# Attention pass of a graph kernel: turned one-hots compared from broadcast offset rows, exponentials also in PSUM, next scores placed earlier on TensorE

## Chip, cores and metric
One core of one Trainium2 chip runs the whole program. The metric is the device time of one execution in microseconds (us). Five engines work side by side: TensorE (PE, its weight loads PEld), VectorE (DVE), ScalarE (ACT), GpSimd (POOL) and SyncE (SP), which issues DMAs.

## What is computed
Four graph layers run on 6250 nodes of 128 features and 200,000 edges sorted by target. Only the third, an attention layer with 4 heads, is changed:

```python
h_src, h_tgt = h[src], h[tgt]
att = jnp.sum(jnp.concatenate([h_src, h_tgt, e], axis=-1) * a, axis=-1)
att = jnp.where(att > 0, att, 0.2 * att)
m = jnp.maximum(segment_max(att, tgt), 0.0)
ex = jnp.exp(att - m[tgt])
denom = segment_sum(ex, tgt) + (num_edges - deg)[:, None] * jnp.exp(-m)
out = segment_sum((ex / denom[tgt])[:, :, None] * h_src, tgt)
```

## The kernel before
`attention_pass` takes the edges in 196 groups of 1024 (128 partitions times J = 8 slots), written out four at a time (U = 4 buffers, so 49 rounds). Targets are sorted, so the targets of a group lie in a window of 128 nodes. Each engine has its own program, and a `step` function says in which order it takes the parts of neighbouring groups. Semaphores tie the engines together. Within step g:

- **POOL** gathers the 1024 source rows of a group by 8 indirect DMAs (L2885). It may refill a buffer when `weigh` has used it (`weighed`), so it gathers group g+3 once group g-1 is weighed, and the group's indices must have been loaded.
- **SP** issues, group by group, the loads of the edge features `e64`, of the window's table `ht` and of the gates `gate` (L2864, L2867, L2869), each waiting until the same buffer's last user four groups earlier is done, and after each round the four index loads (L1195).
- **ACT** makes the one-hots "edge i has target w" in `make_hots` fashion three groups ahead: 8 instructions of distances, one Relu to bf16 (`hots`, L3247), a widening to f32 (`widen_hots`, L3256). It copies the turned one-hots out of PSUM (`take_hots`, L3265) and the turned edge features (`take_edges`, L3273), takes the sums (`take_sums`, L3300), and makes the exponentials (`weights`, L3292).
- **PE** turns the one-hots (`turn_hots`, L3106), multiplies turned edges and one-hots into scores (`score_edges`, L3131 and L3133), turns the run ends and the carries (`turn_ends`, `turn_carries`), and sums the weighted rows of the last group in two halves (`sum_rows`, L3171).
- **DVE** adds the parts of a score, runs the segmented maxima, carries them over partitions, subtracts, and in `weigh` (L3065) multiplies the gathered rows by the exponentials.

PE's order in a step is: first half of the last group's sums, run ends, second half of those sums, carries, scores of the next group, turned edges and one-hots of the group after, scale, sums turned. DVE's order ends with differences, `close_tops`, `sum_scores(nxt)` (L2922, waits for the next group's scores) and `weigh(g)`. ACT's order is: edges and one-hots of the next group, half of the distances, `take_sums(last)`, `weights(g)`, then the rest.

`weights_stage` prepares weights early in the program, long before. `Passes` keeps a window's offsets.

## Time and profile before

| | us |
|---|---|
| median of 3 runs | 7490.35 (7471.94 to 7496.29) |
| the profiled execution's own time | 7530.3 |
| its span | 7528.5 |
| the attention pass in it, from its first sums to its last (L3171) | 3863.4 to 6571.4 |

In the rows, a time at the start of a line of the timeline is us from the span's start, the second number is the busy time of that row, and square brackets hold the idle time of the engine just before it with what ended it. "remote" stands where the event that ended a wait could not be put down to an instruction's end. "issue" means that nothing the profile shows was waited for. PE records carry the modelled end of the arithmetic, not the moment when the semaphore was seen by others.

### The profile page before, as it was taken

How to read it: one execution, taken by the hardware profiler on the slowest of the kernel's cores; microseconds unless marked ns; L12 is line 12 of the kernel's file. 1: busy time of each engine (PE TensorE's matmuls, PEld its weight loads, DVE VectorE, ACT ScalarE, POOL GpSimd, SP SyncE). 2: the span in 40 equal slices, each digit the busy share in tenths (PEclk: the TensorE clock that was granted, in tenths of full speed). 3: DMA queues.
4: the chain of work that ended last, by engine and by line, in shares of the span. 5: the costliest groups of instructions: out<-in, count | busy, mean ns of one | idle time of the engine just before them, and what ended most of it. 6: DMA issues, size and time to landing. Idle time of an engine off the chain costs nothing. (4 is left out here: it accounts for less than half of the span.)

```text
span 7528.5 us, 95690 instructions
## 1 busy us (share of the span) xinstructions
PE 4397.0 (58%) x27040; PEld 3669.2 (49%) x27040; DVE 2592.7 (34%) x8505; ACT 2302.1 (31%) x5410; POOL 4035.3 (54%) x4085
## 2 busy tenths in 40 slices
PE   3288883445544555544445655565655655548887
PEld 2155552445544545544434544555554554435555
DVE  5876553111111111111244333333333433441214
ACT  0233443111111111111144544444444444420002
POOL 0266653566666666666345555555555555446660
PEclk6599995777777777777756566656656556669896
DMA  3133332111111111111122222222222222144441
GB/s 54 38 117 128 137 127 72 42 46 48 45 44 44 48 46 47 46 43 45 29 58 58 57 63 56 62 58 57 63 56 62 58 57 61 44 131 138 143 144 38
DMA packets 363838, 510.15 MB, mean 68 GB/s; under 512 B 200192, under 2 KB 258774, under 8 KB 352657
## 3 DMA queue, kind: packets, MB, share of 16 engines
q0 software_dynamic: 129536, 268.78, 14.3%
q1 hardware_dynamic: 234137, 239.31, 10.4%
q8 instruction: 87, 1.43, 0.1%
q14 instruction: 78, 0.64, 0.0%
HBM read 416.50 MB, written 91.05 MB: 67 GB/s over the span
## 5 line engine op out<-in xcount | busy, mean ns | idle before, releaser
L2885 POOL DMA_INDIRECT rows_l<-table,idx_l x1568 | 1496.8, 955 | 1255.1 <-issue 1028.2
L2527 POOL DMA_INDIRECT rows_l<-table,idx_l x1568 | 1565.2, 998 | 918.1 <-issue 761.9
L3171 PE MATMUL p_sum_l<-wrow_l,hot_l 128*128 128x136 f32 x3136 | 789.5, 430 | 1092.0 <-DVE wrow_l L3065 1092.0
L2663 PE MATMUL ps_l<-hoty_l,rows_l 128*128 128x144 f32 x3136 | 688.3, 399 | 1147.2 <-DVE hoty_l L2595 863.5
L3171 PEld LDWEIGHTS p_sum_l<-wrow_l,hot_l 128*128 128x128 f32 x3136 | 717.4, 325 | 1186.8 <-issue 871.3
L1475 POOL DMA_INDIRECT rows_l<-table,row_idx x896 | 934.1, 1043 | 543.4 <-issue 250.9
L2663 PEld LDWEIGHTS ps_l<-hoty_l,rows_l 128*128 128x128 f32 x3136 | 631.2, 284 | 1190.1 <-DVE hoty_l L2595 653.0
L2611 DVE TENSOR_TENSOR acc<-acc,pw_l 128x128 f32 x196 | 56.6, 289 | 2048.4 <-DMA counts_table<-h_nodes 1157.6
L2549 ACT COPY agg_l<-ps_l 128x432 f32<-128x432 f32 (+1 forms) x588 | 276.0, 479 | 1436.3 <-PE ps_l L2663 849.7
L2676 PE MATMUL pm_l<-w_mix,agg_l 128*128 128x128 f32 x3528 | 517.1, 307 | 43.2 <-issue 42.9
L2676 PEld LDWEIGHTS pm_l<-w_mix,agg_l 128*128 128x128 f32 x3528 | 501.9, 225 | 48.9 <-issue 46.6
L3236 ACT ACTIVATE apart_l<-iota,rel_s_l 128x128 bf16<-128x128 f32 x1568 | 497.2, 387 | 10.1
L1730 PE MATMUL pa_l<-pieces_l,x_nodes 128*128 128x384 bf16 x2254 | 453.6, 338 | 26.2 <-issue 23.9
L1730 PE MATMUL pa_l<-pieces_l,h_nodes 128*128 128x384 bf16 x2156 | 432.6, 339 | 28.6 <-issue 23.0
L2922 DVE TENSOR_REDUCE score_l<-bank_s_l 128x32 f32<-128x128 f32 x196 | 57.4, 293 | 1112.0 <-remote 1102.8
L1716 PE MATMUL pc_l<-hot_key_l,hot_lo_l 128*128 128x392 bf16 (+1 forms) x1152 | 288.2, 313 | 195.4 <-issue 81.3
L1730 PEld LDWEIGHTS pa_l<-pieces_l,x_nodes 128*128 128x128 bf16 x2254 | 223.7, 101 | 177.5 <-issue 54.3
L1591 DVE TENSOR_TENSOR hot_lo_l<-lo_iota_l,tile_lo 128x512 bf16<-128x512 bf16 x288 | 198.6, 690 | 323.8 <-PE pc_l L1716 246.1
L1730 PEld LDWEIGHTS pa_l<-pieces_l,h_nodes 128*128 128x128 bf16 x2156 | 214.5, 101 | 180.5 <-issue 56.4
L1593 DVE TENSOR_SCALAR hot_key_l<-key_iota_l,key_l 128x392 bf16<-128x392 f16 (+1 forms) x1152 | 291.7, 307 | 0.0
L2595 DVE TENSOR_TENSOR hoty_l<-hot_l,y_l 128x1152 f32<-128x1152 f32 x196 | 266.5, 1360 | 13.2 <-PE ps_l L2663 6.5
L2560 ACT COPY msg_l<-pm_l 128x128 f32<-128x128 f32 x196 | 52.6, 268 | 711.5 <-DMA x_nodes<-in_x 394.1
(552 smaller groups left out, 7041.3 us busy)
## 6 DMA issues: line engine op xcount, KB each, us to landing
rows_l<-table,idx_l POOLq DMA_INDIRECT x3136
e_l<-in_edge_attr SPq DMA_DIRECT2D x196, 256.0 KB
counts_table<-x_nodes SPq DMA_DIRECT2D x22, 1568.0 KB
x_nodes<-counts_table SPq DMA_DIRECT2D x22, 1568.0 KB
counts_table<-h_nodes SPq DMA_DIRECT2D x21, 1568.0 KB
h_nodes<-counts_table SPq DMA_DIRECT2D x21, 1568.0 KB
rows_l<-table,row_idx POOLq DMA_INDIRECT x896
raw_l<-in_edge_attr SPq DMA_DIRECT2D x49, 144.0 KB
```

What stands on the lines that cost most here:

```text
L1475: pool.indirect_dma_start(out=rows[:, slot, j, :], out_offset=None, in_=table, in_offset=bass.IndirectOffsetOnAxis(ap=what[:, j:j + 1], ax ...
L1593: nc.vector.tensor_scalar(hot_key[:, f % RING, 0:near_keys], key_iota[:, 0:near_keys], key[:, t:t + 1], None, ALU.is_equal).then_inc(tile_ ...
L1716: nc.tensor.matmul(pc[m % BANKS][:, at:at + near_keys], hot_lo[:, f % RING, :], hot_key[:, f % RING, 0:near_keys], start=(k % per == 0), s ...
L1730: last = nc.tensor.matmul(pa[n % 2][:, 0:PIECES * D], counts[n % BUFFERS][:, a, :], pieces[:, a, :, :].rearrange("p k d -> p (k d)"), star ...
L2527: pool.indirect_dma_start(out=rows[:, u, j, :], out_offset=None, in_=table, in_offset=bass.IndirectOffsetOnAxis(ap=idx[:, u, j:j + 1], axi ...
L2549: nc.scalar.copy(agg[:, s, :, a:b, :], ps[n][:, 0:(b - a) * Y * RANGE].rearrange("p (t c d) -> p c t d", c=Y, d=RANGE)).then_inc(part_take ...
L2595: nc.vector.tensor_tensor(hoty[:, s, :, :, :], hot[:, s, :, :].unsqueeze(2).broadcast_to([P, J, Y, RANGE]), y[:, :, u * J:(u + 1) * J].rea ...
L2663: last = nc.tensor.matmul(ps[n][:, at:at + Y * RANGE], rows[:, u, t, :], hoty[:, s, t, :, :].rearrange("p c d -> p (c d)"), start=True, st ...
L2676: last = nc.tensor.matmul(pm[s][:, 0:D], agg[:, s, c, :, :].rearrange("p t d -> p (t d)"), w_mix[:, c, :], start=(c == 0), stop=(c == Y - 1))
L2885: pool.indirect_dma_start(out=rows[:, u, j, :], out_offset=None, in_=table, in_offset=bass.IndirectOffsetOnAxis(ap=idx[:, u, j:j + 1], axi ...
L3171: last = nc.tensor.matmul(p_sum[:, 0:WROW], hot[:, s, j, :], wrow[:, s, j, :], start=(j == 0), stop=(j == J - 1))
L3236: last = nc.scalar.activation(apart[:, j, :], core.iota[:, :], ACT.Abs, scale=-1.0, bias=rel_s[:, g.s, j:j + 1])
```

## The change
The turned one-hots no longer come from PE. `weights_stage` once turns the targets' offsets (13 PE transposes into PSUM, ACT copies to 16-bit integers, two DMAs) into a table `rel_rows` in DRAM, one row of 1024 numbers per group. SP loads a group's row into all 128 partitions, and DVE compares it with each partition's own line number, which gives the turned one-hots at once. ACT's bf16 one-hots, the widening copy and the copy of turned ones go, and the one-hots are written once in f32, one group ahead. The exponentials are written twice, first into PSUM for `weigh`, then into the rows for the sums. PE makes the scores of the next group and the carries before the second half of the last group's sums.

```diff
# weights_stage
+        rel = sb("rel_kept", [P, T])
+        rel_row = sb("rel_row", [P, len(chunks), P], I16)
+        pr = ctx.enter_context(nc.psum_tensor("pr", [P, 4, 512], F32))
...
+            sp.wait_ge(rel_taken, START + 1)
+            rows = core.rel_rows.rearrange("g (j p) -> (g j) p", p=P)
+            sp.dma_start(rows[0:full * P, :].rearrange("(c k) p -> k c p", k=P), rel_row[:, 0:full, :]).then_inc(rel_stored, DMA)
+            sp.dma_start(rows[full * P:T, :], rel_row[0:T - full * P, full, :]).then_inc(rel_stored, DMA)
             sp.wait_ge(loaded, START + n * DMA)
+            sp.wait_ge(rel_stored, START + 2 * DMA)
...
+            nc.vector.tensor_scalar(rel[:, :], core.rel0[:, :, :].rearrange("p g j -> p (g j)"), -1.0, None, ALU.max).then_inc(rel_kept, 1)
...
+            for c, (at, k) in enumerate(chunks):
+                turned = nc.tensor.transpose(pr[0:k, c // 4, c % 4 * P:c % 4 * P + P], rel[:, at:at + k], core.ident[:, :])
# Passes
+        link(nc.vector.tensor_tensor(self.mine[:, :], self.line_far[:, :], self.off[:, :], ALU.add))
...
+        nc.vector.tensor_tensor(self.line_far[:, :], core.line[:, :], core.order[:, 1:2], ALU.subtract)
# attention_pass
-        hot_b = sb("hot_b", [P, U, J, WIN], BF16)
+        rel_row = sb("rel_row", [P, J * P], I16)
-        p_hotT = ctx.enter_context(nc.psum_tensor("p_hotT_l2", [P, J, P], BF16))
+        p_ex = psum("p_ex", 512)
+        ex = p_ex[:, 0:2 * Q].rearrange("p (s j h) -> p s j h", s=2, h=H)
# SP, for each u
                     sp.dma_start(gate[:, u, :, :], core.gates[ds(rnd * U + u, 1), :, :].broadcast_to([2 * H, 4, P])
                                  ).then_inc(gate_loaded[u], DMA)
+                    sp.wait_ge(hotT_made[u - 1], START + t + (u > 0))
+                    sp.dma_start(rel_row[:, :], core.rel_rows[ds(rnd * U + u, 1), :].broadcast_to([P, J * P])).then_inc(row_loaded[u], DMA)
# DVE
+            def make_turned_hots(g):
+
+                if g is None:
+                    return
+                dve.wait_ge(row_loaded[g.u], START + g.t * DMA + DMA)
+                if g.near(-2):
+                    dve.wait_ge(scored[g.near(-2).u], START + g.near(-2).t + 1)
+                nc.vector.tensor_scalar(hotT[:, g.s, :, :], rel_row[:, :].rearrange("p (j e) -> p j e", e=P), win.mine[:, :], None,
+                                        ALU.is_equal).then_inc(hotT_made[g.u], 1)
...
                                         rows[:, u, :, 0:D].rearrange("p j (h c) -> p j h c", h=H),
-                                        wrow[:, s, :, D:ROW].unsqueeze(3).broadcast_to(wide), ALU.mult).then_inc(weighed[u], 1)
+                                        ex[:, s, :, :].unsqueeze(3).broadcast_to(wide), ALU.mult).then_inc(weighed[u], 1)
...
                     sum_scores(nxt)
                     weigh(g)
+                    make_turned_hots(at(2))
# PE
                 if g is None and nxt:
                     turn_edges(nxt)
-                    turn_hots(nxt)
                 sum_rows(last, 0, HALF)
                 turn_ends(g)
+                score_edges(nxt)
+                turn_carries(g)
                 sum_rows(last, HALF, J)
-                turn_carries(g)
-                score_edges(nxt)
                 turn_edges(after)
-                turn_hots(after)
                 turn_scale(last)
                 turn_sums(last)
# ACT
-                nc.scalar.activation(hot_b[:, g.u, :, :], apart[:, :, :], ACT.Relu, scale=-1.0,
-                                     bias=core.one[:, :]).then_inc(hot_b_ready, 1)
+                nc.scalar.activation(hot[:, g.s, :, :], apart[:, :, :], ACT.Relu, scale=-1.0,
+                                     bias=core.one[:, :]).then_inc(hot_ready, 1)
...
-                nc.scalar.activation(wrow[:, s, :, D:ROW], diff[:, s, :].rearrange("p (h j) -> p j h", j=J), ACT.Exp).then_inc(ex_ready, 1)
+                nc.scalar.activation(ex[:, s, :, :], diff[:, s, :].rearrange("p (h j) -> p j h", j=J), ACT.Exp).then_inc(ex_ready, 1)
+                nc.scalar.activation(wrow[:, s, :, D:ROW], diff[:, s, :].rearrange("p (h j) -> p j h", j=J), ACT.Exp).then_inc(ex_kept, 1)
...
                 def step(at):
-                    g, nxt, last, ahead = at(0), at(1), at(-1), at(3)
+                    g, nxt, last = at(0), at(1), at(-1)
...
                     take_edges(nxt)
-                    take_hots(nxt)
-                    copy_rel(ahead, w_)
-                    distances(ahead, 0)
+                    copy_rel(nxt, w_)
+                    distances(nxt, 0)
                     take_sums(last)
                     weights(g)
                     scales(g, w_)
-                    distances(ahead, 1)
-                    hots(ahead)
-                    widen_hots(g)
+                    distances(nxt, 1)
+                    hots(nxt)
```

## Rows read from the trace of the kernel before
**Rows 1.** The page: busy time of each engine, then two of its costliest groups.
```profile
PE 4397.0 (58%) x27040; PEld 3669.2 (49%) x27040; DVE 2592.7 (34%) x8505; ACT 2302.1 (31%) x5410; POOL 4035.3 (54%) x4085
...
L2885 POOL DMA_INDIRECT rows_l<-table,idx_l x1568 | 1496.8, 955 | 1255.1 <-issue 1028.2
L2527 POOL DMA_INDIRECT rows_l<-table,idx_l x1568 | 1565.2, 998 | 918.1 <-issue 761.9
```
**Rows 2.** Waits in the attention pass (total us, times, longest us).
```profile
DVE score_l L2922 <- remote: 1102.8, 191, 7.6
PE p_sum_l L3171 <- DVE wrow_l L3065: 1092.0, 194, 7.6
POOL rows_l L2885 <- issue: 1023.7, 1505, 11.1
ACT eT_l L3273 <- remote: 445.9, 180, 11.2
```
**Rows 3.** Timeline of one group (start, us, engine, instruction, idle before).
```profile
5005.49 1.22 DVE L3065 TENSOR_TENSOR wrow_l<-rows_l,wrow_l 128x1024 f32<-128x1024 f32 x1
...
5007.48 0.94 POOL L2885 DMA_INDIRECT rows_l<-table,idx_l  x1 [4.25 <-issue]
...
5009.12 0.42 PE L3145 MATMUL p_ends_l<-ident,run_l 128*8 128x128 f32 x1
...
5009.33 2.02 PE L3171 MATMUL p_sum_l<-wrow_l,hot_l 128*128 128x136 f32 x8
...
5011.37 0.20 PE L3157 MATMUL p_back_l<-ident,carried_l 4*128 4x4 f32 x1
...
5012.41 0.34 PE L3133 MATMUL bank_s_l<-ht_l,hotT_l 128*128 128x12 bf16 x8
...
5012.65 0.26 ACT L3292 ACTIVATE wrow_l<-diff_l 128x32 f32<-128x32 f32 x1 [0.99 <-issue]
...
5016.24 0.94 POOL L2885 DMA_INDIRECT rows_l<-table,idx_l  x1 [0.30 <-issue]
5019.09 0.29 DVE L2922 TENSOR_REDUCE score_l<-bank_s_l 128x32 f32<-128x128 f32 x1 [6.33 <-remote]
...
5019.22 0.33 SPq L2867 DMA_DIRECT2D ht_l<-table_t  x1
5019.30 1.22 DVE L3065 TENSOR_TENSOR wrow_l<-rows_l,wrow_l 128x1024 f32<-128x1024 f32 x1
```
**Rows 4.** Timeline of the tensor pass, the end of a long run of gathers.
```profile
2400.54 0.39 PE L2687 MATMUL pw_l<-hot_place_l,msg_l 128*128 128x128 f32 x2
...
2409.91 0.95 POOL L2527 DMA_INDIRECT rows_l<-table,idx_l  x1 [0.30 <-issue]
...
2414.13 0.27 ACT L2560 COPY msg_l<-pm_l 128x128 f32<-128x128 f32 x1 [15.38 <-DMA x_nodes<-in_x]
```
**Rows 5.** Groups by form, nearest kin of the new DVE work (count, busy us, mean ns).
```profile
L1593 DVE TENSOR_SCALAR hot_key_l<-key_iota_l,key_l 128x392 bf16<-128x392 f16 x576 | 160.5, 325 | 0.0
L1593 DVE TENSOR_SCALAR hot_key_l<-key_iota_l,key_l 128x196 bf16<-128x196 f16 x512 | 113.2, 285 | 0.0
...
L1601 DVE TENSOR_TENSOR hot_l<-iota,rel_l 128x1024 f32<-128x1024 f32 x60 | 72.9, 1217 | 0.0
...
L2131 DVE TENSOR_TENSOR a_n<-pt_n,em_n 128x896 f32<-128x896 f32 x7 | 7.6, 1086 | 0.1
```
**Rows 6.** The page: gathers of the first layer's pass, beside which DVE does L1593.
```profile
L1475 POOL DMA_INDIRECT rows_l<-table,row_idx x896 | 934.1, 1043 | 543.4 <-issue 250.9
```
**Rows 7.** Timeline: two SP issues without gathers, index loads, their gather; DMA time to landing.
```profile
3895.80 0.35 SPq L2864 DMA_DIRECT2D e_l<-in_edge_attr  x1
...
3897.15 0.33 SPq L2867 DMA_DIRECT2D ht_l<-table_t  x1
...
5026.10 8.48 SPq L1195 DMA_DIRECT2D idx_l<-in_src  x3
...
5050.18 0.94 POOL L2885 DMA_INDIRECT rows_l<-table,idx_l  x1 [4.15 <-DVE wrow_l L3065]
...
ht_l<-table_t SPq DMA_DIRECT2D x192, 3.0 KB, 1.5
```

More of the change, by code:

```diff
@@ L23 @@
 I32 = mybir.dt.int32
+I16 = mybir.dt.int16
 ALU = mybir.AluOpType
@@ L200, in __init__ @@
         self.tops_off = sb("tops_off", [P, 1])
+        self.line = sb("line_no", [P, 1])
+        self.rel_rows = nc.dram_tensor("rel_rows", (sh.groups, J * P), I16, kind="Internal").ap()
         self.passes = sb("passes", [1, 3], I32)
@@ L2299, in weights_stage @@
 def weights_stage(nc, core, w, a):
+    sh = core.sh
     with ExitStack() as ctx:
@@ L2312, in weights_stage @@
         pn = ctx.enter_context(nc.psum_tensor("pn", [P, 512], F32))
+        T = sh.groups * J
+        chunks = [(at, min(P, T - at)) for at in range(0, T, P)]
+        full = T // P
+        rel = sb("rel_kept", [P, T])
+        rel_row = sb("rel_row", [P, len(chunks), P], I16)
+        pr = ctx.enter_context(nc.psum_tensor("pr", [P, 4, 512], F32))
+        rel_kept = sem("rel_kept")
+        rel_turned = sem("rel_turned")
+        rel_taken = sem("rel_taken")
+        rel_stored = sem("rel_stored")
         zeroed = sem("zeroed")
@@ L2371, in _ @@
         def _(act):
+            act.wait_ge(rel_turned, START + 1)
+            for c in range(0, len(chunks), 4):
+                n = min(4, len(chunks) - c)
+                if c + n > full:
+                    n -= 1
+                    taken = nc.scalar.copy(rel_row[0:T - full * P, full, :], pr[0:T - full * P, full // 4, full % 4 * P:full % 4 * P + P])
+                if n:
+                    taken = nc.scalar.copy(rel_row[:, c:c + n, :], pr[:, c // 4, 0:n * P].rearrange("k (c p) -> k c p", p=P))
+            taken.then_inc(rel_taken, 1)
             nc.scalar.copy(w.ident_b[:, :], core.ident[:, :])
@@ L2377, in _ @@
         def _(pe):
+            pe.wait_ge(rel_kept, START + 1)
+            for c, (at, k) in enumerate(chunks):
+                turned = nc.tensor.transpose(pr[0:k, c // 4, c % 4 * P:c % 4 * P + P], rel[:, at:at + k], core.ident[:, :])
+            turned.then_inc(rel_turned, 1)
             pe.wait_ge(zeroed, START + 3)
@@ L2715, in __init__ @@
         self.wipe = ctx.enter_context(nc.sbuf_tensor(f"wipe_{tag}", [P, 1], F32))
+        self.line_far = ctx.enter_context(nc.sbuf_tensor(f"line_far_{tag}", [P, 1], F32))
+        self.mine = ctx.enter_context(nc.sbuf_tensor(f"mine_{tag}", [P, 1], F32))
         self.ready = sems_of.new(f"windows_ready_{tag}")
@@ L2823, in attention_pass @@
         gate_loaded = sems("gate_loaded", U)
+        row_loaded = sems("row_loaded", U)
+        hotT_made = sems("hotT_made", U)
         group_begun = sem("group_begun")
@@ L2836, in attention_pass @@
         summed_score = sem("summed_score")
+        ex_kept = sem("ex_kept")
         weighed = sems("weighed", U)
@@ L3043, in differences @@
                 if g.near(-2):
-                    dve.wait_ge(ex_ready, START + g.near(-2).k + 1)
+                    dve.wait_ge(ex_kept, START + g.near(-2).k + 1)
                 nc.vector.tensor_tensor(diff[:, s, :], score[:, s, :], top[:, :, :].rearrange("p h j -> p (h j)"),
@@ L3071, in step @@
                     g, nxt, old = at(0), at(1), at(-2)
+                    if g is None and nxt:
+                        make_turned_hots(nxt)
                     add_sources(g)
@@ L3096, in _ @@
             windows = win.count(pe)
-            def turn_hots(g):
-                if g is None:
-                    return
-                pe.wait_ge(hot_b_ready, START + g.k + 1)
-                if g.near(-1):
-                    pe.wait_ge(hotT_ready, START + g.near(-1).k + 1)
-                for j in range(J):
-                    last = nc.tensor.transpose(p_hotT[:, j, :], hot_b[:, g.u, j, :], w.ident_b[:, :])
-                last.then_inc(hot_turned, 1)
             def turn_edges(g):
@@ L3125, in score_edges @@
                 pe.wait_ge(eT_ready, START + g.k + 1)
-                pe.wait_ge(hotT_ready, START + g.k + 1)
+                pe.wait_ge(hotT_made[u], START + g.t + 1)
                 pe.wait_ge(ht_loaded[u], START + g.t * DMA + DMA)
@@ L3167, in sum_rows @@
                     pe.wait_ge(weighed[u], START + g.t + 1)
+                    pe.wait_ge(ex_kept, START + g.k + 1)
                     if g.near(-1):
@@ L3233, in distances @@
                     if g.near(-1):
-                        act.wait_ge(hot_b_ready, START + g.near(-1).k + 1)
+                        act.wait_ge(hot_ready, START + g.near(-1).k + 1)
                 for j in range(half * HALF, (half + 1) * HALF):
@@ L3300, in take_sums @@
                 nc.scalar.copy(sums[:, g.s, :], p_sum[:, 0:WROW]).then_inc(sums_copied, 1)
-            def make_hots(g, w_):
-                copy_rel(g, w_)
-                distances(g, 0)
-                distances(g, 1)
-                hots(g)
             with act.Fori(0, windows) as w_:
                 def step(at):
-                    g, nxt, last, ahead = at(0), at(1), at(-1), at(3)
-                    if g is None and nxt:
-                        make_hots(nxt, w_)
-                        make_hots(at(2), w_)
+                    g, nxt, last = at(0), at(1), at(-1)
                     take_edges(nxt)
-                    take_hots(nxt)
-                    copy_rel(ahead, w_)
-                    distances(ahead, 0)
+                    copy_rel(nxt, w_)
+                    distances(nxt, 0)
                     take_sums(last)
```

26 lines of the change are left out of this document (6 added, 20 removed).

## The prediction
> **What bounds the kernel now.** The page's busy shares come first [rows 1]: PE has 58% and POOL 54% of the span, so no engine is full, and what counts is who waits for whom. The gathers of the attention pass (L2885) are busy 1496.8 us and idle 1255.1 us, together 14.0 us for each of 196 groups. About 10.0 us of that is the gather's own pace, 8 instructions that start 1.25 us apart. The waits view [rows 2] says where the rest is: DVE waits 1102.8 us in 191 groups, 5.8 us each, for `scored`, and PE 1092.0 us for the weighed rows that DVE makes right after.
>
> The timeline of one group [rows 3] shows a ring. `weigh` ends at 5006.71 (5005.49 + 1.22). POOL starts the next gather 0.77 us later, and its last instruction ends at 5017.18, 9.70 us on. DVE's `sum_scores` starts 1.91 us after that and `weigh` ends at 5020.52, 1.43 us further. The four pieces are 13.81 us, and the next group repeats them. That PE's score matmuls ended at 5012.75 (5012.41 + 0.34), 6.3 us before DVE went on, is the strange part. SP, which waits for the same semaphore, goes on at 5019.22 too. So not DVE is late, the signal is. Earlier signals of the same step were on time: run ends (5009.54) and carries (5011.57), 2.1 and 4.1 us after the gather began, and the exponentials at 5012.65 stand on the carries. I read this as a rule of this trace: a PE signal that is raised up to 4.1 us into a run of gathers passes, one raised at 5.3 us is held until 1.9 us after the last gather instruction. The tensor pass has it too [rows 4]: PE ends at 2400.93, the last gather instruction at 2410.86, and ACT goes on at 2414.13. The rows do not say what holds the signal.
>
> **The change part by part.** Times below are counted from the end of the last group's `weigh` (5006.71).
>
> *One-hots.* PE loses 8 transposes, ACT two copies. Nobody waits for them: PE stands idle 1092.0 us in the pass [rows 2], so I take nothing for their loss. DVE gains one comparison of 128x1024, 16-bit in and out. Its kin [rows 5] take 285 ns at 196 columns and 325 ns at 392, 0.20 ns a column, so 0.45 us at 1024; the other bound is the f32 comparison of the same size, 1.22 us. I take 0.45 us because the kin is a 16-bit comparison with a number per partition. It lies behind `weigh` and ahead of `add_sources`, and PE covers it: the run ends are turned only after the first half of the sums, at 2.2 us, while the scans, now ready at about 1.1 us, would be ready at 1.55. At 1.22 us they would be 0.1 to 0.3 us late.
>
> The comparison ends before POOL's first gather instruction at 0.77 us. The nearest view of the two side by side is the first layer's pass [rows 6]: 1043 ns for a gather there, beside the 16-bit comparisons, against 955 ns here. By that difference on one gather it costs 0.09 us a group at most, 17 us in all, an upper bound that I leave to the range.
> The Trainium skill (SBUF — State Buffer, SBUF: two separate sides) says that a DVE operation in a two-port mode locks GpSimd out, so that it cannot write descriptors. By it the comparison would stop POOL for its whole length if they met, 0.45 us a group or 88 us in all; the row above shows a fifth of that at most.
>
> *Exponentials.* One more ACT instruction (0.26 us [rows 3]) behind the one that `weigh` waits for. It hides in ACT's idle time. `weigh` reading PSUM costs the same as before: 1086 ns for 896 columns out of PSUM [rows 5] is 1.21 ns a column, and L3065 has 1.19 [rows 3]. No row shows ACT writing to PSUM, so I take 0.26 us with 0.1 us to either side.
>
> *Order on PE.* The next scores now follow the run ends (2.83 us). They took 5011.57 to 5012.75, 1.2 us, and up to 2 us at the lower clock, so `scored` is raised at 3.9 to 4.7 us, that is 3.1 to 3.9 us into the gather, early enough to pass. The carries keep their place near 4.9 us, bound by DVE's scans. What is pushed back is the second half of the sums, 2.02 us [rows 3]. It used to end at 4.64 us and now ends near 6.9 us, 6.1 us into the gather: that is where the scores stood before, and their signal never passed. ACT's `take_sums(last)` waits for it, and `weights(g)` stands behind `take_sums` in ACT's program. So what is late next is the sums' signal: it is held to 12.4 us like the scores now. After it come `take_sums` (0.2 us until the next ACT instruction), the exponentials 0.26, a start 0.07 and `weigh` 1.22, 1.75 us in place of 1.43. That is +0.32 us a group, +63 us.
>
> *SP.* The new row load waits for `hotT_made` of the group before, since there is one buffer. That puts SP close behind DVE. It comes to a round's index loads only after the last group's row load, thus after `weigh` of the group three earlier and its comparison, at 0.5 us. Now the index loads are issued at 5026.10 and used at 5050.18, 24 us ahead [rows 7]. After the change they are issued when POOL wants them: 0.5 us, 1.35 us for issuing a 256 KB load (from its start to that of the next issue [rows 7]), 1.5 us until a small load lands [rows 7], 0.77 us for POOL to start, so the gather begins at 4.1 us and not at 0.77. Once a round the ring is 3.3 us late. That is not given back: the group's own signals do pass then and its `weigh` comes at about 8.6 us, but the next gather follows at once, the double run ends at 23.8 us, its signals come at 25.7, and from run ends to `weigh` it is another 5.8 us (carries 2.0, sums 2.0, then 1.75). That is 31.5 us for two groups where 28.2 were due, again +3.3 us. 48 rounds give +158 us; the bounds are 0, if some signals pass during the double run, and 160.
>
> *Start.* `weights_stage` gets two more stores and their landing behind its loads, 2 x 0.33 plus 1.5 us [rows 7], +2 us; its transposes and copies run beside SP's issuing.
>
> **Sum.** 7530.3 + 2 + 63 + 158 = 7753 us for the profiled execution. It was 40 us above the median of the runs, so the forecast is 7713 us, rounded to 7710.
>
> **The rivals.**
> 1. *Signals leak through the run of gathers.* In the tensor pass POOL's ring is built alike, and a group costs (1565.2 + 918.1) / 196 = 12.67 us [rows 1], so some signals do pass there. If the earlier scores let the attention pass run like that, it gains (13.81 - 12.67) x 196 = 223 us: 7270 us. For it: the scores are the longest wait, and they do move in front of the limit. Against it: the sums take their old place to within 0.3 us.
> 2. *Only the scores' signal is ever held.* Then `weigh` ends at 8.6 us, POOL's pace of 10.0 us sets the ring, and 3.8 us x 196 = 745 us go: 6750 us. The tensor pass, where another signal is held for 13 us [rows 4], speaks against it.
> 3. *It changes nothing that can be measured.* The sums' signal is held, but the exponentials' tail or the index loads give back what they cost. 7480 to 7510 us.
> 4. *The carries are held as well* (the other end of my own case). If SP's denser issuing brings the limit below 3.9 us, the chain from the carries follows the release: 1.1 us to the exponentials (5011.57 to 5012.65 [rows 3]), then 0.26, 0.07 and 1.22, 2.6 us in place of 1.43. That is 1.2 us a group more instead of 0.32, 7530 + 2 + 235 + 158 - 40 = 7885 us. This decides once carries are raised later than the limit.
>
> **How the numbers follow.** My case has 0.50, its own range is 7540 (no loss by the index loads, +0.32 us) to 7830 (a comparison at 1.22 us or some carries held). Rival 1 has 0.20, rival 2 0.16, rival 3 0.10, rival 4 0.04. A difference under 0.3%, 22 us, is about what a measurement of this kernel cannot tell from none. Slower by more than that: 0.54; within: 0.10; faster: 0.36. The range for 8 in 10 runs from below rival 1 (7200 us) to 7830; it leaves out rivals 2 and 4.
>
> **What the profile after would show.** If I am right, DVE's wait before `sum_scores` (L2922) is gone, ACT waits 5 us a group in front of `take_sums` with "remote" beside it, its start stays 1.9 us behind the last gather instruction, and the steps repeat every 14.1 us. Every fourth gather starts some 4 us after `weigh`, and SP's index loads are issued less than 3 us ahead of it. The gathers' idle time in the pass is above 1255 us. I am wrong if `take_sums` starts within 0.1 us of PE's last sum in most groups, or if POOL's gaps between groups shrink below a microsecond: then the gathers' pace is the limit and the kernel is faster. If the index loads are still issued many microseconds early, my second term falls and the forecast is 7550 us.

## The result and the profile after the change

The changed kernel takes **7729.77 us** (median of 4 runs, 7705.9 to 7799.84) against 7493.32 us for the kernel before, measured beside it: a ratio of 1.0309, 95% interval 1.0206 to 1.0412. It is slower, and the forecast of 7710 us lies 20 us from it. The profiled execution is the run of 7705.9 us, the shortest of the four. That is the answer for the chip of these runs. The experiments below show that on two other chips the sign is the other way, and why.

The page of the changed kernel, the lines that answer to [rows 1], and the group that has become ScalarE's longest wait:

```profile
PE 4418.3 (57%) x25485; PEld 3661.7 (48%) x25485; DVE 2669.1 (35%) x8706; ACT 1943.5 (25%) x5218; POOL 4059.4 (53%) x4085
...
L2929 POOL DMA_INDIRECT rows_l<-table,idx_l x1568 | 1505.3, 960 | 1474.2 <-issue 935.3
L2561 POOL DMA_INDIRECT rows_l<-table,idx_l x1568 | 1575.2, 1005 | 873.0 <-issue 778.6
...
L3328 ACT COPY sums_l<-p_sum_l 128x136 f32<-128x136 f32 x196 | 53.4, 273 | 1871.6 <-remote 953.1
```

ACT lost 359 us of work and PE 1555 instructions. POOL gathers the same 1568 times in the attention pass, but it is idle 1474.2 us ahead of them where it was 1255.1: +219 us, and that is the loss. The trace says the same by the weighings: the first ends at 3833.4 us and the last at 6756.1, 2922.8 us, where the kernel before has 3863.4 to 6568.0, 2704.6 us: +218. What lies ahead of the first became 30 us shorter and what lies behind the last 12 us, which leaves +176 us between the two profiled executions.

The waits view of the attention pass, to be set beside [rows 2] (total us, times, longest us). "remote" and "issue" are read as there:

```profile
ACT sums_l L3328 <- remote: 947.8, 87, 16.2
POOL rows_l L2929 <- issue: 921.2, 1473, 9.4
ACT sums_l L3328 <- PE p_sum_l L3218: 853.9, 90, 19.4
...
DVE lifts_l L3083 <- remote: 576.4, 97, 7.6
DVE from_left_l L3036 <- remote: 551.8, 57, 15.9
POOL rows_l L2929 <- DMA idx_l<-in_src: 499.8, 47, 14.1
```

DVE's 1102.8 us in front of `sum_scores` is gone. In its place ACT waits for the sums, DVE for the carries (`lifts`), and 47 times, once in nearly each of the 49 rounds, POOL waits for an index load.

The timeline of one group, and further down of the place where a round ends (start, us, engine, instruction, idle before), to be set beside [rows 3] and [rows 7]:

```profile
5015.17 1.22 DVE L3119 TENSOR_TENSOR wrow_l<-rows_l,p_ex_l 128x1024 f32<-128x1024 f32 x1
...
5017.17 0.95 POOL L2929 DMA_INDIRECT rows_l<-table,idx_l  x1 [6.67 <-issue]
...
5019.44 0.34 PE L3179 MATMUL bank_s_l<-ht_l,hotT_l 128*128 128x12 bf16 x8
...
5020.86 0.20 PE L3203 MATMUL p_back_l<-ident,carried_l 4*128 4x4 f32 x1
...
5020.99 1.19 PE L3218 MATMUL p_sum_l<-wrow_l,hot_l 128*128 128x136 f32 x8
...
5025.92 0.94 POOL L2929 DMA_INDIRECT rows_l<-table,idx_l  x1 [0.30 <-issue]
5025.93 0.22 DVE L3083 TENSOR_TENSOR lifts_l<-ends_of_l,p_back_l 128x64 f32<-128x64 f32 x1 [4.70 <-issue]
...
5028.70 0.27 ACT L3328 COPY sums_l<-p_sum_l 128x136 f32<-128x136 f32 x1 [8.97 <-remote]
5028.87 0.23 ACT L3319 ACTIVATE p_ex_l<-diff_l 128x32 f32<-128x32 f32 x1
...
5029.14 1.22 DVE L3119 TENSOR_TENSOR wrow_l<-rows_l,p_ex_l 128x1024 f32<-128x1024 f32 x1 [1.97 <-ACT p_ex_l L3319]
...
5043.96 1.22 DVE L3119 TENSOR_TENSOR wrow_l<-rows_l,p_ex_l 128x1024 f32<-128x1024 f32 x1
5045.09 0.48 DVE L3064 TENSOR_SCALAR hotT_l<-rel_row_l,mine_l 128x1024 bf16<-128x1024 int16 x1
...
5045.74 0.34 SPq L2914 DMA_DIRECT2D rel_row_l<-rel_rows  x1
5046.35 2.05 SPq L1199 DMA_DIRECT2D idx_l<-in_src  x4
...
5049.95 0.95 POOL L2929 DMA_INDIRECT rows_l<-table,idx_l  x1 [9.12 <-DMA idx_l<-in_src]
```

Two things are to be read here. PE's last sum of the group ends at 5022.18 (5020.99 + 1.19). ACT, which waits for it, copies at 5028.70, 6.5 us later and 1.84 us after the last gather instruction's end (5026.86). The exponentials and the weighing come behind that copy. And at the end of a round the weighing ends at 5045.18, the comparison at 5045.57, then SP issues the row load, then the four index loads. The gather that needs them begins at 5049.95, 4.77 us after the weighing, where [rows 3] has 0.77.

The group shown is not the only kind of step. Of the 195 steps from weighing to weighing, 64 are over 20 us (two groups' gathers in one run), 66 are under 10 us (nearly all of them the step just ahead of a long one), and 65 lie between, 14.4 us in the mean. Nearly every round has one long step, and 16 of the 49 have a second one.

### The profile page after: what moved, and what is told of

Its sections match the earlier page's. It is cut to its first block and busy times, and to the rows that moved or that the text cites. A ratio compares the mean times of both kernels' runs of the same rounds, so it can differ in the third digit from the quotient of the medians.

```text
span 7704.1 us, 92797 instructions
## 1 busy us (share of the span) xinstructions
PE 4418.3 (57%) x25485; PEld 3661.7 (48%) x25485; DVE 2669.1 (35%) x8706; ACT 1943.5 (25%) x5218; POOL 4059.4 (53%) x4085
## 3 DMA queue, kind: packets, MB, share of 16 engines
q1 hardware_dynamic: 263961, 291.11, 12.5%
q8 instruction: 87, 1.43, 0.1%
## 5 line engine op out<-in xcount | busy, mean ns | idle before, releaser
L2929 POOL DMA_INDIRECT rows_l<-table,idx_l x1568 | 1505.3, 960 | 1474.2 <-issue 935.3
L3218 PEld LDWEIGHTS p_sum_l<-wrow_l,hot_l 128*128 128x128 f32 x3136 | 671.4, 306 | 254.3 <-issue 250.9
L3328 ACT COPY sums_l<-p_sum_l 128x136 f32<-128x136 f32 x196 | 53.4, 273 | 1871.6 <-remote 953.1
L3202 PE MATMUL p_back_l<-ident,carried_l 4*128 4x4 f32 x196 | 47.7, 243 | 806.5 <-issue 437.3
L3202 PEld LDWEIGHTS p_back_l<-ident,carried_l 4*128 4x128 f32 x196 | 34.1, 174 | 816.2 <-issue 814.5
L3177 PEld LDWEIGHTS bank_s_l<-w_edge,eT_l 128*128 128x128 f32 x1568 | 318.4, 300 | 77.0 <-issue 41.8
L3177 PE MATMUL bank_s_l<-w_edge,eT_l 128*128 128x8 f32 x1568 | 307.8, 325 | 47.3 <-issue 26.2
L3036 DVE TENSOR_TENSOR_SCAN from_left_l<-gate_l,from_left_l,p_ends_l 8x128 f32<-8x128 bf16 x196 | 91.9, 469 | 641.3 <-remote 551.8
```

The source lines that it names most:

```text
L2929: pool.indirect_dma_start(out=rows[:, u, j, :], out_offset=None, in_=table, in_offset=bass.IndirectOffsetOnAxis(ap=idx[:, u, j:j + 1], axi ...
L3177: nc.tensor.matmul(p_score[:, 2 * j:2 * j + 2, PARTS:PARTS + H], eT[:, j, :], w.edge[:, :], start=True, stop=True)
L3218: last = nc.tensor.matmul(p_sum[:, 0:WROW], hot[:, s, j, :], wrow[:, s, j, :], start=(j == 0), stop=(j == J - 1))
```

## The experiments

Below, "the hold" is what the prediction read from the trace: a signal of PE that is raised during a run of gathers reaches the engine that waits for it several us later. Twelve runs were made on three chips, each beside the kernel before. I call the chips by order: A (at two times), B and C. The kernel before takes 6176 and 6190 us on A, 6202 us on B and 7466 us on C. The times and profile that this case started from (7490 us) look like C.

### Four variants made for the hold

The first four variants were chosen to take the predicted terms away one at a time, or to set one up alone. In the changed kernel, `two_rows` gives the row load two buffers:

```
-        rel_row = sb("rel_row", [P, J * P], I16)
+        rel_row = sb("rel_row", [P, 2, J * P], I16)
...
-                    sp.wait_ge(hotT_made[u - 1], START + t + (u > 0))
+                    sp.wait_ge(hotT_made[u - 2], START + t + (u > 1))
```

> The changed kernel with two buffers for the offset row, so that SP's row load waits one group less far. My theory: the index loads are issued 14 us or more before POOL wants them, no gather starts later than 0.8 us after its weigh, the steps of 8.6 and 21.9 us become steps of 14.0 to 14.9, mean period 14.2 in place of 15.0 us, and the time falls by about 150 us to 7580. The rival, that the extra 256 KB load a group or the extra DVE instruction is what costs: the period stays near 15.0 and the time within 30 us of the changed kernel.

`sums_later` swaps two lines of ACT's program in the changed kernel:

```
-                    take_sums(last)
                     weights(g)
+                    take_sums(last)
```

> The changed kernel with ACT's take_sums behind weights instead of ahead of it, index loads as late as in the change. My theory: the held signal of the sums no longer stands before the exponentials, so a group whose carries pass is weighed 8 us after the last; the gathers then join into runs of two groups, the run ends of the second group are held, and two groups take about 27 us: 13.5 a group, 7440 us, with up to 100 us more for the late index loads. The rival, that the sums are not what holds the step: the period stays at 15.0 us.

`both_mended` has both edits.

> Both edits: two row buffers and take_sums behind weights. My theory: runs of two groups of gathers, 27 us for two groups, 13.4 to 13.5 a group, 7430 to 7450 us, thus about as fast as the kernel before or 50 us faster. The rival, that only one signal in a step is ever held: then nothing is left that waits, a group takes POOL's 10.0 us and the time is below 6900 us.

`order_alone` is the kernel before with PE's new order and nothing else:

```
-                sum_rows(last, HALF, J)
-                turn_carries(g)
                 score_edges(nxt)
+                turn_carries(g)
+                sum_rows(last, HALF, J)
```

> The kernel before with PE's new order alone (scores of the next group and carries before the second half of the sums). My theory: sum_scores waits no more, take_sums waits until 1.9 us after the last gather instruction, period 14.1 us, in one group of four 14.9 where the carries are held too, mean 14.3, thus 7490 + 100 = 7590 us, ratio 1.008 to 1.015. The rival, that the earlier scores help and the loss of the change lies in its loads: ratio below 1, scores seen early and the step shorter than 13.8 us.

Measured on chip A, where the kernel before takes 6175.75 us: `two_rows` 6136.28 us (ratio 0.9932, interval 0.9915 to 0.9949), `sums_later` 6126.96 (0.9924, 0.9908 to 0.9941), `both_mended` 6127.51 (0.9922, 0.9905 to 0.9938), `order_alone` 6241.63 (1.0111, 1.0094 to 1.0128).

None of the expected differences between the first three can be seen, because the thing they rest on is missing. In the four traces not one signal of PE comes 1.8 to 2.15 us after a last gather instruction, and there is no last one: POOL issues 1568 gathers without a single pause over 0.5 us. The mean step from weighing to weighing is 10.01 to 10.03 us in the first three and 10.67 us in `order_alone`. So the hold that my whole sum is made of belongs to something outside the kernel. These runs don't confirm the forecast's terms. `order_alone` falls inside its expected ratio (1.008 to 1.015) by luck: the hold from which that was worked out isn't there. They ask two new questions: whether the hold goes with the chip, and what makes 10.01 of one kernel and 10.67 of another when the gathers pace both.

### The unmodified kernels on another chip

> The changed kernel, unchanged, timed beside the kernel before on one chip. If the hold of TensorE's signals behind the gathers belongs to the chip and not to the kernel: where the trace of before taken there shows no signal released 1.8 to 2.15 us after the last gather, the changed kernel shows none either and takes some 6130 us, 0.7 per cent under before, a mean of 10.0 us a group paced by the 9.7 us of gathers. Where it shows them (before near 7490 us), 7730 us again. If instead the change itself brings the slow ring (the single buffer and the sums ahead of the weights), it takes over 6250 us where before takes 6176, since neither of the two mended versions' 6127 to 6136 says anything of it.

> The kernel before, for its profile on the chip of these runs. If it is the missing hold that makes it 6176 us: mean 10.0 to 10.2 us a group, first gather within 1 us of the weighing's end, no signal released 1.8 to 2.15 us after the last gather (175 of 196 in the profile shown before), and the instructions' own durations the same within 2 per cent (gathers 0.96 us, weighing 1.22 us). If it is a faster chip all round: the gathers and the vector instructions shorter by some 18 per cent, the ratio of 6176 to 7490.

`after_old_order` is the changed kernel with PE's order put back (the reverse of the diff of `order_alone`).

> The changed kernel with TensorE's order as it was (sums, carries, scores of the next group). Without the hold: if the new order costs by itself (1.1 per cent in the kernel before, where the second half of the sums came later and with them ScalarE's copy ahead of the weights) then this is faster than the changed kernel or equal to it where the gathers pace both, 6125 to 6135 us. If the new order is what the change gains by, this is slower than the changed kernel, 6160 us or more. With the hold: 7560 us, since the sums are off the held signals but the row's single buffer still delays one gather start in four.

> The changed kernel with ScalarE's weights ahead of its copy of the sums, once more, for the case that the chip of these runs shows the hold. Without the hold 6127 us again, a mean of 10.0 us a group. With the hold: 13.5 us a group in the steps that start their gathers at once, some 7600 us in all; by the rival that the held signals come to the same whatever the order, 7730 us.

Measured on chip B, before 6202.3 us: `after_again` 6130.82 us (ratio 0.9895, interval 0.9853 to 0.9937), `before_again` 6214.7 us (one run), `after_old_order` 6125.15 us (0.9884, 0.9843 to 0.9924), `sums_later_again` 6128.29 us (one run). **Without the hold the change makes the kernel faster, by 1.05%.** PE's order makes no difference in the changed kernel (6131 and 6125 us) although it cost 1.1% in the kernel before.

The gathers of the attention pass on the page, first `before_again`:

```profile
L2885 POOL DMA_INDIRECT rows_l<-table,idx_l x1568 | 1595.8, 1018 | 511.4 <-issue 475.7
```

then `after_again`:

```profile
L2929 POOL DMA_INDIRECT rows_l<-table,idx_l x1568 | 1501.7, 958 | 510.7 <-issue 476.4
```

The idle time is the 0.30 us between two instructions in both, so POOL is the bound, and all of the gain is in the instructions themselves: 1595.8 - 1501.7 = 94 us. By the weighings the pass went from 2047.1 us (first end 3334.4, last 5381.5) to 1951.8 us (3334.3 to 5286.0): 95 us. Something makes gathers of the kernel before longer that the change took away. `before_again` also answers its own question. The weighing takes 1.22 us and the shortest gathers 0.94 us on every chip, so B is not a faster chip: what it lacks is the wait. Its mean step is 10.50 us, above the 10.0 to 10.2 that I had expected, and its gathers are 1.02 us in the mean, not 0.96. The granted clock isn't what differs either: `after_again` has 0.62 of full speed in the pass and no hold, the trace before has 0.63 and the hold. Nor are the gathers' transfers slower where the hold is: their packets take 14.3% of 7528.5 us there and 17.3% of 6212.9 us in `before_again`, 1077 and 1075 us. A timeline from it:

```profile
4299.07 1.22 DVE L3065 TENSOR_TENSOR wrow_l<-rows_l,wrow_l 128x1024 f32<-128x1024 f32 x1
4299.42 1.68 POOL L2885 DMA_INDIRECT rows_l<-table,idx_l  x1 [0.30 <-issue]
...
4307.43 0.34 PE L3133 MATMUL bank_s_l<-ht_l,hotT_l 128*128 128x12 bf16 x8
...
4307.81 0.29 DVE L2922 TENSOR_REDUCE score_l<-bank_s_l 128x32 f32<-128x128 f32 x1 [0.28 <-PE bank_s_l L3133]
4308.02 1.22 DVE L3065 TENSOR_TENSOR wrow_l<-rows_l,wrow_l 128x1024 f32<-128x1024 f32 x1
...
4308.94 1.12 POOL L2885 DMA_INDIRECT rows_l<-table,idx_l  x1 [0.30 <-issue]
```

The scores' signal, raised at 4307.77 in the middle of the gathers, is there at 4307.81: no hold. And the gather that starts at 4299.42, inside a weighing that ends at 4300.29, takes 1.68 us and not 0.94. The one at 4308.94 meets the last 0.30 us of a weighing and takes 1.12 us.

Grouped over the whole pass, by how much of the weighing was left when a gather started (us; count of gathers, mean length of them):

```
                 left 0-0.3      0.3-0.6       0.6-0.9       0.9-1.22     sum over 0.945 us
before_again     41, 1.00        55, 1.27      64, 1.57      34, 1.92      93 us
order_alone      11, 1.01        23, 1.29      98, 1.57      62, 1.84     126 us
after_again      70, 0.94        58, 0.95      38, 0.94      28, 0.94       0 us
```

The 8 more gathers of `before_again` that start within 0.03 us of the weighing's start take 0.95 us in the mean. A gather that starts during the weighing is stopped until about the weighing's end; one that starts together with it hardly, and one that is already running when the weighing starts is not touched. `order_alone` differs from `before_again` only in where in the gathers' beat the weighing falls: more of its 194 meetings come early in the weighing. In the changed kernel gathers meet the weighing as often, and none is stopped. The edit that looks like the cause is the operand: the weighing reads its factors from PSUM. The next runs test it.

### The operand alone

`ex_psum_alone` is the kernel before with the exponentials in PSUM and nothing else. A bank was made free by putting `p_back` into the second half of the bank of `p_ends`.

```
+        ex = p_ex[:, 0:2 * Q].rearrange("p (s j h) -> p s j h", s=2, h=H)
...
-                                        wrow[:, s, :, D:ROW].unsqueeze(3).broadcast_to(wide), ALU.mult).then_inc(weighed[u], 1)
+                                        ex[:, s, :, :].unsqueeze(3).broadcast_to(wide), ALU.mult).then_inc(weighed[u], 1)
...
-                nc.scalar.activation(wrow[:, s, :, D:ROW], diff[:, s, :].rearrange("p (h j) -> p j h", j=J), ACT.Exp).then_inc(ex_ready, 1)
+                nc.scalar.activation(ex[:, s, :, :], diff[:, s, :].rearrange("p (h j) -> p j h", j=J), ACT.Exp).then_inc(ex_ready, 1)
+                nc.scalar.activation(wrow[:, s, :, D:ROW], diff[:, s, :].rearrange("p (h j) -> p j h", j=J), ACT.Exp).then_inc(ex_kept, 1)
```

> The kernel before with one part of the change alone: exponentials also into PSUM, and the weighing reads them there. Its bank comes from putting the carries' bank beside the run ends'. One-hots, their transposes, the load order and TensorE's order stay as they were. Theory of the port: all of the change's gain, mean step 10.0 us, 6105 to 6135 us (without the 5 us of the new rows' making), overlapping gathers 0.945. Rival, gain from the freed TensorE and ScalarE: no gain, 6200 us, the gathers at 0.945 only if they no longer meet the weighing. If the chip holds the signals: 7490 us as before.

`ex_sbuf` is the reverse: the changed kernel, with the weighing reading `wrow` again and ACT writing that copy first.

> The changed kernel, but the weighing reads its exponentials from SBUF again (ScalarE still writes both copies, the SBUF one first). Theory: where the gathers run back to back, the weighing with all operands in SBUF stops the gather that it meets, as in the kernel before (361 gathers that overlap it: 1.204 us in the mean against 0.962), and the change took this away (0.945 of 364 overlapping). Then the overlapping gathers are 1.2 to 1.35 us again, the mean step 10.4 to 10.65 instead of 10.01, the time 6210 to 6250 us against 6131 for the changed kernel. Rival: the 71 us come from the work taken from TensorE and ScalarE (transposes of one-hots and their copies), then the time stays at 6130 and the gathers at 0.945. If the chip holds TensorE's signals behind the gathers, weighing and gathers hardly meet (2 of 1568 in the trace before) and it takes 7730 us.

Measured on chip A, before 6189.97 us: `ex_psum_alone` **6117.14 us** (ratio 0.9886, interval 0.9869 to 0.9902), `ex_sbuf` 6161.44 us (0.9954, 0.9940 to 0.9969). The page of `ex_psum_alone`:

```profile
L2888 POOL DMA_INDIRECT rows_l<-table,idx_l x1568 | 1498.6, 956 | 510.1 <-issue 471.7
```

and its timeline:

```profile
4299.06 1.21 DVE L3068 TENSOR_TENSOR wrow_l<-rows_l,p_ex_l 128x1024 f32<-128x1024 f32 x1
4299.19 0.94 POOL L2888 DMA_INDIRECT rows_l<-table,idx_l  x1 [0.30 <-issue]
```

The gather starts 0.13 us into the weighing, with 1.08 us of it left, and takes 0.94 us. None of its 191 meetings with a weighing makes a gather longer. The one edit gives all of the gain that the change has where there is no hold (1.14% on A, against 1.05% for the whole change on B). It is settled in this direction: beside it, the transposes and copies taken from PE and ACT, the comparison, the row load and PE's order give nothing more there. The page of `ex_sbuf`:

```profile
L2929 POOL DMA_INDIRECT rows_l<-table,idx_l x1568 | 1535.2, 979 | 510.9 <-issue 475.8
```

It loses 1535.2 - 1501.7 = 34 us of the 94, and 31 us by the medians, though on different chips. I had expected 80 to 120 us. The mechanism held and the size was off: 140 of its 201 meetings come when less than 0.3 us of the weighing is left, so the stops are short (the same count as above gives 37 us). The phase in which the ring settles is not the kernel before's, and I had taken it over from there.

### What paces it without the hold

`half_gathers` is the changed kernel with four gathers to a group. The other half of the rows is not loaded: it holds zeros.

```
-                        for j in range(J):
+                        for j in range(HALF):
```

> The changed kernel with four of the eight gathers of a group left out, so half of the rows are zeros or old; all else is as it was. If the gathers pace the pass on this chip (8 x 1.25 = 10.0 us a group, no pause over 0.5 us between 1568 gathers), the mean step falls to the ring's own, 7.3 to 8.9 us (the short steps of the runs so far are 7.3 to 8.9), and the time to 5690 to 5920 us. If something with a period of its own (SyncE's loads, TensorE at its clock) also stands at 10.0, the time stays near 6130. If the chip holds the signals: the run of gathers is 5.0 us, within the reach of a held signal only just, a step of 8.6 to 9.1 us, some 6450 us in all because the passes around are held too.

Measured on chip A: 5766.06 us (one run; before 6189.97). Its page:

```profile
L2932 POOL DMA_INDIRECT rows_l<-table,idx_l x784 | 761.1, 971 | 852.7 <-issue 472.7
```

The mean step is 8.21 us, from 3330.2 to 4930.4 us. So with half of the gathers the ring goes 1.8 us a group faster, and in the full kernel the 8 gathers at 1.25 us are the bound. That fits `two_rows`, `sums_later` and `after_old_order` coming to nearly the same, 6125 to 6136 us: each shortens a ring that already waits for POOL.

### The two mends where the hold is

> The changed kernel with two buffers for the row and ScalarE's weights ahead of its copy of the sums, in case its chip shows the hold. If the kernel before takes some 7490 us there (the hold): the gathers start 0.8 us after the weighing in every step and the sums are no longer ahead of the weights, so a step is 0.78 + 9.70 + 1.90 + 1.1 = 13.5 us, a gain of 0.3 us a group on the kernel before, 7430 us; by the rival that other held signals (the ring's carries, in the steps that start late) come next, 7490 to 7600 us. If the kernel before takes 6170 to 6200 us there (no hold): 6127 us again, a mean step of 10.0 us, paced by the gathers.

Chip C has the hold: the kernel before takes 7466.11 us (7399.49 to 7541.65, 7 runs). `both_mended` takes 7504.11 us there (7481.0 to 7591.39), a ratio of 1.0117 with an interval of 0.9998 to 1.0236. The expected 7430 us was too good. Its waits in the attention pass:

```profile
DVE lifts_l L3083 <- remote: 953.3, 149, 17.3
POOL rows_l L2929 <- issue: 942.7, 1518, 10.6
...
POOL rows_l L2929 <- DVE wrow_l L3119: 278.4, 47, 8.9
```

and one step of its timeline:

```profile
4769.22 0.94 POOL L2929 DMA_INDIRECT rows_l<-table,idx_l  x1 [3.58 <-issue]
...
4772.91 0.20 PE L3203 MATMUL p_back_l<-ident,carried_l 4*128 4x4 f32 x1
...
4777.95 0.95 POOL L2929 DMA_INDIRECT rows_l<-table,idx_l  x1 [0.30 <-issue]
4779.31 0.22 DVE L3083 TENSOR_TENSOR lifts_l<-ends_of_l,p_back_l 128x64 f32<-128x64 f32 x1 [6.03 <-remote]
4780.24 0.23 ACT L3319 ACTIVATE p_ex_l<-diff_l 128x32 f32<-128x32 f32 x1 [8.14 <-issue]
4780.51 1.22 DVE L3119 TENSOR_TENSOR wrow_l<-rows_l,p_ex_l 128x1024 f32<-128x1024 f32 x1
4780.68 0.27 ACT L3328 COPY sums_l<-p_sum_l 128x136 f32<-128x136 f32 x1
```

The two mends do what they were made for. The index loads no longer make POOL late, the sums' copy comes behind the exponentials, and the pass takes 2692.6 us (3855.7 to 6548.3), where the changed kernel's profile has 2922.8: by the profiles both losses together, 230 us, are taken back. The two chips need not be the same one, so the size is rough. By the ratios, each taken beside the kernel before, less comes back: 1.031 becomes 1.012. The two edits were not run apart where the hold is, so how the loss divides between the sums and the index loads rests on the trace of the changed kernel alone. What comes next is the carries: raised at 4773.11, 3.9 us after the gathers began, seen by DVE at 4779.31, 0.4 us after their end. The median step is 13.3 us, 0.2 us under the 13.5 that I had worked out. But in 16 rounds a group passes without its hold (8.2 us), and the next comes at 21.4 us, behind two groups' gathers; the mean is 13.81 us, against 13.87 in the trace before. This version does not beat the kernel before on C by any interval, and the rival of my expectation, that the carries come next, is what the waits show.

`ex_psum_alone`, the best version on chips without the hold, was not run on C. Where the hold is, it should take what the kernel before takes, since in that trace one gather of 1568 starts inside a weighing; this is argued and not shown.

## Why the prediction was right

**The hold and the ring.** Right for the chip of the result. The trace before was read as a ring of 13.81 us in which the scores' signal comes 1.91 us after the last gather instruction, and the changed kernel has its release at 1.84 us in the group shown. But the rule that I drew, "up to 4.1 us into a run passes, 5.3 us is held", was read from one group and is wrong in its own trace. The waits view of the kernel before has this line, which I had passed over:

```profile
DVE lifts_l L3029 <- remote: 156.7, 56, 3.7
```

There, in 56 groups, the carries are raised 3.5 to 4.1 us into the run and wait 1.8 to 3.6 us, until 2.4 to 4 us before the last gather instruction's end. In most of the others they are raised as late, up to 4.2 us, and pass at once. The row of the tensor pass [rows 4] goes on 3.3 us after the last gather instruction, not 1.9, and the view puts its wait down to a DMA, so it is a weak witness for the same rule. In the trace after, the carries are raised at 5021.06, 3.9 us after the gather began, and DVE goes on at 5025.93, held for 4.9 us. On chip C the same signal, also 3.9 us in, waits 6.2 us. So time since the start of the gathers is not what decides, and the release has no one place either. In the two changed versions PE has raised the scores' signal just ahead of the carries, and there they wait far more often (97 and 149 times). Whether a signal that is held takes the later ones with it is open; it can't be all of it, since the kernel before raises the scores behind the carries and has 56 such waits.

**The sums take the place of the scores.** Right in the group shown, and in part over the pass; this was the main step. Forecast: released at 12.4 us after the weighing, then 1.75 us in place of 1.43, a step of 14.1 us. Measured in the rows above: 5028.70 - 5016.39 (the end of the last weighing, at 5015.17 + 1.22) = 12.31 us, then 1.66 us, a step of 13.97 us. The parts of it were near enough: the exponential into PSUM 0.23 us (0.26 taken), the weighing 1.22 (1.22). What the step had wrong is that the carries would pass. In the 65 steps of 13 to 15 us the sums are seen at 12.3 or 12.5 us (the medians of the two kinds), as forecast, but the carries are held there too, and in 57 of these steps the exponentials start right behind the differences that stand on the carries. In 32 of the 65 that costs next to nothing (a median step of 14.05 us); for the other 32 see the next paragraph. So with the sums out of the way the carries hold the ring at nearly the same length, which is what `both_mended_again` shows.

**The index loads.** Right, and a little better than its parts. Forecast: a gather start 4.1 us after the weighing, a step of 8.6 us, then 22.9 us behind the double run, 31.5 us for two. Measured: 4.77 us in the row at 5049.95 (the index loads issued 3.6 us ahead of it, where under 3 was said), median steps of 8.61 and 21.91 us, 30.5 us for two. The remaining step was taken as 14.13 us like the others and has a median of 14.86, because in 32 rounds the carries come at 12.4 us there, as late as the sums, and the exponentials, which wait for what stands on them, start 0.9 us behind the sums' copy: the mechanism of rival 4, to which I gave 0.04. Such a round is 59.4 us in the median where the working gives 31.5 + 2 x 14.13 = 59.8. In the other 16 rounds these two steps are a second short and long one, 8.8 and 21.6 us, which the working did not have, and the round takes 61.2 us in the mean. The trace doesn't say what makes every third round do so.

**The sum.** +63 and +158 us in the pass, 221 together, against +218 measured. This is closer than the parts deserve, and partly luck: one is 1 us a round too long, another 0.7 too short, and the second long pair was not foreseen. For the profiled execution the sum says 7753 us and it took 7705.9, 47 less: 42 of these are time outside the pass, 30 us ahead of it and 12 behind, which the two profiled executions differ by and the sum doesn't have. It is the correction of 40 us to the median that brings the forecast near, though this profiled execution lies 24 us below its median and not above. The 2 us at the start can't be told from those 30. Two slips in the working change nothing here: the low end of the forecast's own range is given as 7540 where its terms give 7555, and the scores' signal as 3.9 us after the weighing where 2.83 + 1.2 is 4.0. It was measured at 3.4.

**The comparison.** 0.45 us taken, 0.48 measured, and covered as said. The stop that the prediction weighed against it is real, but seldom met. In `after_old_order` a gather that starts 0.1 us into the comparison, with 0.39 us of it left, takes 1.20 us, and one with 0.21 us left takes 1.03: it stands until 0.13 us before the comparison's end. In `after_again` only 38 gathers of 1568 start during a comparison, most of them near its end or together with it, and they lose 3 us in all, not 88.

**Exponentials, costed at nothing.** This is the step that holds only where the hold is. I compared the length of the weighing with one operand in PSUM and in SBUF, found it equal (it is, 1.22 us and 1.22 us), and stopped. What changed was another engine's time. The row for it could not be in that trace: its gathers start 0.77 us after the weighing, and just one of 1568 begins inside a weighing (it took 1.17 us). On A and B the gathers never pause, meet the weighing, and the same edit is worth 73 us (6190 to 6117).

The Trainium skill (SBUF — State Buffer, SBUF: two separate sides) says that DVE and GpSimd share a port pair as an exclusive lock, which is taken also by a DVE operation with two SBUF inputs against a GpSimd operation that reads SBUF, and that the one which comes second is fully blocked. The runs agree: 1.57 us for a gather with 0.6 to 0.9 us of an all-SBUF weighing left, 0.94 us with one operand in PSUM, and no effect on a gather that was first (159 of them in `before_again`, 0.95 us). That the gather instruction counts as such a GpSimd operation is what these runs add. I had weighed this rule against the new comparison, for which it would matter little, and not against the operation from which the change takes an SBUF input.

**The rivals.** Rival 2, the scores' signal alone held and POOL's pace of 10.0 us as the bound, has the step that A and B show, but not for its reason: there is no hold there at all, before or after, so the 3.8 us a group are no gain of the change.

## What to carry to other kernels

Before costing a change to a kernel whose waits say "remote" and end at a fixed distance behind another engine's run, find out whether this wait is there on another chip: here the same kernel takes 6176 to 6202 us on two and 7466 us on a third, and the change makes it 1% faster without the wait and 3% slower with it. Read such a wait in all groups and not in one. When an operand of a long VectorE operation moves between SBUF and PSUM, read the lengths of GpSimd's instructions beside it and not only the operation's own. A single buffer for a load puts everything behind it in its queue at the mercy of its consumer: here the row load's wait for the last comparison moved the index loads from 24 us ahead of their gather to 3.6 us ahead, too late.

## What the runs showed of the hardware

- Whether PE's signals are held during back-to-back gathers differs between chips for one and the same kernel: none on A and B. In the trace before, the run ends' signals, raised 2 us into a run, pass, those of the carries at 3.5 to 4.2 us are held in 56 of 196 groups, and the scores at about 5.2 us wait in 191. In the changed kernel's trace carries raised about 4 us in wait 7 us in the median. The release has no one place: 2.4 to 4 us before the end of the run's last instruction for those 56 carries, 1.8 to 2.15 us after it for the scores in 175 groups, and up to 3.4 us after it in the changed kernel. The hold goes with 1260 to 1290 us of this kernel (7466 against 6176 and 6202), while a weighing (1.22 us) and the shortest gathers (0.94 us) are the same. What makes the difference is not settled, and C was used at one time only, so the chip can't be told from the occasion.
- A gather instruction (0.945 us) that starts while VectorE multiplies 128x1024 f32 from two SBUF operands is stopped until about the end of that operation and takes up to 2.0 us in all. With one operand in PSUM it is not, and a gather that started first isn't either.
- The comparison of 128x1024, int16 in and bf16 out, both in SBUF (0.48 us), stops a gather in the same way: the 38 to 40 gathers that it visibly stops in `sums_later` and in `after_old_order` wait until 0.13 us before its end. Where the two start within 0.1 us of each other the gather keeps 0.94 us and the comparison takes up to 0.55.
- What such meetings cost depends on the phase in which the two engines lock: 93, 126 and 37 us in `before_again`, `order_alone` and `ex_sbuf`, with 194 to 202 meetings each. That is part of why a new order on PE cost 66 us in the kernel before and nothing in the changed one: the stops cost 126 us with it, and 93 us without it on chip B. There is no profile of the kernel before on A, so the rest is open.
